# A graph layer on one core: edge blocks of 512 for a node range, and ten paired pairs in two regions

## What is computed

```python
h = relu(layernorm(x))                       # x: 3125 nodes x 64
msg = concat(h[dst], edge_attr)              # 53125 edges, sorted by dst
m = relu(msg @ W1a.T + b1a) @ W1b.T + b1b    # 128 hidden
agg = segment_sum(m, src) / max(count(src), 1)
z = relu(concat(h, agg) @ W2a.T + b2a) @ W2b.T + b2b
out = x + concat(z, h) @ Wr.T + br
```

## Time and profile before

| | us |
|---|---|
| time, median of 3 runs | 522.17 (521.17 to 524.77) |
| span of the profiled execution | 518.3 |
| TensorE busy | 431.0 (83%) |
| GpSimd busy | 356.1 (69%) |
| VectorE busy | 298.0 (57%) |
| ScalarE busy | 285.0 (55%) |
| moved by DMA | 123.45 MB, mean 238 GB/s |

### The profile page before, as it was taken

One profiled execution on the slowest core, in us unless ns is written; L12 is line 12 of the kernel. 1 busy time (PEld: TensorE's weight loads), 2 busy tenths in 40 slices (PEclk: granted clock), 3 DMA queues, 4 the chain that ended last, 5 costly groups with the idle time before them and its releaser, 6 DMA issues.

```text
span 518.3 us, 9203 instructions
## 1 busy us (share of the span) xinstructions
PE 431.0 (83%) x3133; PEld 390.0 (75%) x3133; DVE 298.0 (57%) x825; ACT 285.0 (55%) x576; POOL 356.1 (69%) x406
## 2 busy tenths in 40 slices
PE   6655988899999999998689779845999787987795
PEld 4555777888796988878578778845998777987674
DVE  7868642534656657555425547414765537667884
ACT  3442957774787777786658378171633772100073
POOL 4777777777677777777777777777777777776000
PEclk9876696987999899988899889986999897999999
DMA  7998998553959477978553989996999997778631
GB/s 182 306 338 229 257 266 271 155 156 108 303 143 294 141 257 265 257 255 263 164 151 92 336 249 333 312 331 196 360 326 336 328 322 221 248 214 256 177 86 43
DMA packets 62319, 123.45 MB, mean 238 GB/s; under 512 B 9369, under 2 KB 33374, under 8 KB 62270
## 3 DMA queue, kind: packets, MB, share of 16 engines
q1 hardware_dynamic: 49598, 91.25, 59.0%
q0 software_dynamic: 12672, 31.58, 18.8%
HBM read 71.53 MB, written 51.25 MB: 237 GB/s over the span
## 4 chain that ended last, share of the span: by engine, by line
POOL 32%; PE 26%; DMA 13%; issue 13%; DVE 7%; ACT 5%; SPq 2%; POOLq 0%; ACTq 0%; DVEq 0%
POOL slots_dram L568 24%; PE bank L1261 10%; POOL pairs_dram L551 8%; DMA slots_dram<-pay,pos_i 7%; PE bank L1241 4%; PE bank L1270 4%; DMA dstb<-in_dst 4%; DVE oh L774 2%; DMA rows<-slots_dram 2%; ACT eo L1059 2%; SPq L475 1%; PE bank L1294 1%; PE bank L1291 1%; PE bank L1211 1%; PE bank L1362 1%
## 5 line engine op out<-in xcount | busy, mean ns | idle before, releaser
L568 POOL DMA_INDIRECT slots_dram<-pay,pos_i x300 | 289.0, 963 | 98.7 <-issue 89.6
L1261 PE MATMUL bank<-rows,oh 128*125 128x130 f32 x1100 | 139.5, 287 | 40.3 <-DVE oh L774 40.1
L1261 PEld LDWEIGHTS bank<-rows,oh 128*125 128x125 f32 x1100 | 133.3, 198 | 44.6 <-issue 43.4
L1059 ACT ACTIVATE eo<-dstb,minus_lane 64x256 f32<-64x256 int32 x190 | 85.1, 494 | 94.5 <-DMA dstb<-in_dst 79.8
L1241 PE MATMUL bank<-pw,eo 128*128 128x128 f32 x856 | 119.9, 299 | 3.5 <-ACT pay L1042 2.3
L1241 PEld LDWEIGHTS bank<-pw,eo 128*128 128x128 f32 x856 | 113.3, 213 | 11.4 <-issue 8.0
L774 DVE TENSOR_TENSOR oh<-bank,rows 128x1500 f32<-128x1500 f32 (+5 forms) x67 | 81.8, 1223 | 17.6 <-DMA rows<-slots_dram 10.4
L1270 PE MATMUL bank<-hid,xch 116*128 116x131 f32 (+1 forms) x512 | 68.3, 294 | 14.6 <-DVE xch L724 8.6
L1270 PEld LDWEIGHTS bank<-hid,xch 116*128 116x128 f32 (+1 forms) x512 | 65.3, 205 | 16.9 <-issue 9.9
L551 POOL DMA_INDIRECT pairs_dram<-pay,pos_c x64 | 61.5, 960 | 22.3 <-issue 18.0
L1064 ACT ACTIVATE eo<-eo,one 64x512 f32<-64x512 f32 x95 | 68.3, 719 | 3.1
(11 more groups left out here) (198 smaller groups left out, 376.7 us busy)
## 6 DMA issues: line engine op xcount, KB each, us to landing
rows<-slots_dram SPq DMA_DIRECT2D x24, 864.0 KB
dstb<-in_dst SPq DMA_DIRECT2D x54, 256.0 KB, 7.7
eo<-in_edges_T SPq DMA_DIRECT2D x54, 256.0 KB, 4.9
rows<-pairs_dram SPq DMA_DIRECT2D x12, 864.0 KB
slots_dram<-zeros SPq DMA_DIRECT2D x9, 756.0 KB, 9.2
slots_dram<-pay,pos_i POOLq DMA_INDIRECT x300
rows<-slots_dram SPq DMA_DIRECT2D x8, 432.0 KB
rows<-slots_dram SPq DMA_DIRECT2D x16, 216.0 KB
```

Of the source, the lines that this page charges most:

```text
L568: pool.indirect_dma_start(out=slots_dram[:, :], out_offset=bass.IndirectOffsetOnAxis(ap=pos_i[:, u, k:k + 1], axis=0), in_=pay[:, u, k, :] ...
L1059: last = A.activation(eo[p, g % EB, a * HB:(a + 1) * HB], dstb[p, g % DB // 2, a * HB:(a + 1) * HB], ACT.Square, bias=minus_lane[p, g // 2 ...
L1261: last = T.matmul(o[0:BN, v * SW:(v + 1) * SW], oh2[:, r % 2, n, :], rows[:, sum_no[r] % RR, n, 0:SW], start=(t == 0), stop=(t == TB[ph] - ...
```

## The change

A window serves a block of 512 edges (462 in a paired pair), so a group has 2 blocks in place of 4: half as many projection matmuls, half as many and twice as long one-hots, window copies of half the size. The windows still hold 64 nodes a group, and begin 18 and 22 nodes ahead in place of 26 and 30. Of the 27 pairs 10 are paired in place of 8, at every other place from pair 4 to pair 22 (g44, g45); three old pairs follow. The paired pairs have two regions of 5 pairs each, with 4 tiles a bucket each, where one region of 6 tiles a bucket was; the phases of old pairs are 5, 5, 3, 2, 1, 1, of 4, 4, 3, 2, 1, 1 tiles a bucket (4, 4, 4, 2, 1, 1 before). The last group has 7 tiles in place of 4. Each region is cleared and checked by itself; the check of a paired region stands behind its last `crank`. The shares of the plan are 25 and -4 in place of 23 and -8.

What the plan gives, counted from the code:

| | before | after |
|---|---|---|
| indirect DMAs, old tiles + paired units | 300 + 64 | 271 + 80 |
| projection matmuls | 108 | 54 |
| hidden matmuls | 428 | 431 |
| sum tiles (of these left over behind g53, without the tail's 25) | 550 (75) | 575 (91) |
| sum rounds left over (and 9 in the tail) | 18 | 20 |
| `h` rounds | g7, 2 in g8, g11, 3 in g12 | g7, 2 in g8, 2 in g9, 2 in g11 |
| `z` rounds | 2 in g12, g15, g19, g23, 2 in g27 | 2 in g11, 5 in g12 |
| sum tiles in groups with a `crank` | g31: 16 | g19: 24, g23: 12, g31: 24, g35: 12, g39: 12, g43: 24 |
| sum tiles in g14 to g37 | 16: 24, 20: 24, 24: 24, 28: 12, 31: 16, 36: 24 | 16: 24, 19: 24, 20: 24, 23: 12, 24: 16, 30: 24, 31: 24, 32: 24, 35: 12, 36: 28 |
| and in g38 to g45 | 39: 12, 40: 24, 41: 24, 42: 16, 43: 24, 44: 24, 45: 24 | 39: 12, 40: 24, 43: 24, 44: 24 |
| and in g46 to g53 | 24, 24, 24, 6, 24, 24, 24, 28 | 0, 13, 27, 27, 24, 24, 24, 24 |

The core of the diff:

```diff
-ORDER = "OOOO" + "CO" * 8 + "O" * 7
+ORDER = "OOOO" + "CO" * 10 + "OOO"
-    WS, HB = 64, 256
+    WS, HB = 64, 512
-    BLOCK = [HB if kind == "O" else UNIT for kind in ORDER]
-    LEAD = [26 if kind == "O" else 30 for kind in ORDER]
+    BLOCK = [HB if kind == "O" else 2 * UNIT for kind in ORDER]
+    LEAD = [18 if kind == "O" else 22 for kind in ORDER]
...
-    PAIRS = [5, 5, 5, 2, 1, 1]
+    PAIRS = [5, 5, 3, 2, 1, 1]
+    PAIRED = [5, 5]
...
-    C = [math.ceil((expected(ph) + 4 * math.sqrt(expected(ph))) / 128) for ph in range(NPH)]
+    C = [math.ceil((expected(ph) + 3.8 * math.sqrt(expected(ph))) / 128) for ph in range(NPH)]
...
-    TB = C + [2 * CT]
+    TB = C + [2 * tiles for tiles in CT]
...
-    AFTER_PHASE = [4, 4, 4, 2, 1, 0, 4]
+    AFTER_PHASE = [4, 4, 3, 2, 1, 0, 4, 3]
...
-    ROUNDS_FROM, FULL_FROM, EARLY_SHARE, SHARE, C_SHARE, MOST = 7, 10, 10, 23, -8, 32
+    ROUNDS_FROM, FULL_FROM, EARLY_SHARE, MOST = 7, 10, 10, 32
+    SHARES = dict(after_old=25, after_paired=-4)
...
+                for p in range(1, NCP):
+                    piece = len(CLEAR_PIECES) - (FIRST_PAIRED[p] - g) // 2
+                    if g % 2 == 0 and 0 <= piece < len(CLEAR_PIECES):
+                        clear_chunks(p, piece)
...
-                        pool.wait_ge(s_cfill, 16 * len(CLEAR_PIECES))
+                        pool.wait_ge(s_cfill[C_STARTS.index(c // 2)], 16 * len(CLEAR_PIECES))
...
-                split_row(c_parts, c_carry, 2 * SCALE * SCALE, S["cw"])
+                if n + 1 not in C_STARTS:
+                    split_row(c_parts, c_carry[:], 2 * SCALE * SCALE, S["cw"])
+                    return
+                p = C_STARTS.index(n + 1) - 1
+                check_chunks(p)
+                if p + 1 < NCP:
+                    split_row(c_parts, c_first[:, p + 1, :], 2 * SCALE * SCALE, S["cw"])
...
-                for c in range(KW):
+                for c in range(blocks_of(i)):
```

More of the change, by code:

```diff
@@ L86, in gnn_layer @@
     CU = UNITS * len(C_GROUPS)
[L87 to L93, removed]
+    c_mean = [2 * UNITS * pairs * (UNIT / NB / 2 + 0.25) for pairs in PAIRED]
+    c_dev = [math.sqrt(2 * UNITS * pairs * (UNIT / NB / 4 + 0.0625)) for pairs in PAIRED]
+    CT = [math.ceil((c_mean[p] + 3.8 * c_dev[p]) / 128) for p in range(NCP)]
+    C_CAP = [tiles * 128 for tiles in CT]
+    C_BEGIN = [CR * UNITS * 128 + NB * sum(C_CAP[:p]) for p in range(NCP)]
+    C_ROOM = [min(C_CAP[p], 32 * math.ceil((C_CAP[p] - c_mean[p] + 4.5 * c_dev[p]) / 32)) for p in range(NCP)]
+    C_LEAST = [C_CAP[p] - C_ROOM[p] for p in range(NCP)]
+    assert all(0 < room <= 256 for room in C_ROOM)
+    C_SLOTS = C_BEGIN[-1] + NB * C_CAP[-1] + CU * 128
+    assert C_SLOTS < 2 ** 15
     HR, PR = 2, 4
@@ L137, in gnn_layer @@
     room = 0
-    for g in range(NG):
+    for g in range(LG):
         units = [("perm", C_GROUPS.index(g - 1), u, 0) for u in range(UNITS)] if g - 1 in C_GROUPS else []
@@ L165, in gnn_layer @@
     round_of = {n: r for r, n in sum_no.items()}
-    first_round = [min(r for r, v in enumerate(rounds) if v[0] == "sum" and v[1] == ph) for ph in range(NPH + 1)]
+    first_round = [min(r for r, v in enumerate(rounds) if v[0] == "sum" and v[1] == ph) for ph in range(NPH + NCP)]
     last_perm = [rounds.index(("perm", c, UNITS - 1, 0)) for c in range(len(C_GROUPS))]
@@ L344, in scatters_of @@
         def scatters_of(u, n):
-            return 16 * sum(KT[O_GROUPS[a]] for a in range(u, n, PB))
+            return 16 * sum(KT[O_GROUPS[a]] for a in range(u, min(n, len(O_GROUPS)), PB))
         def chunk_scatters_of(u, c):
@@ L460, in _ @@
             loaded = 0
-            for g in range(3, NG):
+            for g in range(3, LG):
                 if g >= 6:
@@ L539, in _ @@
             count(unit_row[:], [[1, K + 1], [0, 2]], 0, 0)
-            count(c_first[:], [[C_CAP, NB]], C_BEGIN, 0).then_inc(S["late"], 1)
+            for p in range(NCP):
+                last = count(c_first[:, p, :], [[C_CAP[p], NB]], C_BEGIN[p], 0)
+            last.then_inc(S["late"], 1)
             pool.wait_ge(S["pad"], 1)
-            for g in range(NG):
+            for g in range(LG):
                 if g in C_GROUPS:
@@ L1098, in _ @@
             copy_window(4)
-            for g in range(3, NG):
+            for g in range(3, LG):
                 relu(g)
-                if g + 2 < NG:
+                if g + 2 < LG:
                     copy_window(g + 2)
@@ L1297, in sum_round @@
                     pe.wait_ge(S["bc"], 1)
[L1298 to L1299 removed]
+                    for a in range(2):
+                        last = T.transpose(o[0:1, a * NBK:(a + 1) * NBK], col_stat[:, a:a + 1], I[0:NBK, 0:NBK])
                 last.then_inc(S["ag"], 1)
```

126 lines of the change are left out of this document (68 added, 58 removed).

## The result

The changed kernel takes 563.36 us (median of 4, 560.58 to 565.31), the kernel before beside it 521.67 (520.62 to 524.77): a ratio of 1.0787, 95% interval 1.0741 to 1.0833. A later run of both gave 1.0836 (1.0766 to 1.0906). Slower, as forecast, but by 42 us and not by 15: 563 lies outside the range of 510 to 547. Times are medians of all runs of a kernel, while ratios leave out single runs that lay over 1.5% above the kernel's fastest, so a ratio can differ from the quotient of the medians, in e16 by 0.9%.

What follows compares the result with a forecast made beforehand. Before, GpSimd's indirect DMAs were taken as the bound; after, TensorE paces: 137.9 + 269.6 + 0.5 = 408.0, GpSimd's last DMA at 492.7, tail 40.3, span 533.0, with 3.9 about 537 us measured. Range 510 to 547.

Steps and rivals of the forecast that it cites:

- what becomes the bound: g14 to g45: TensorE paces eight cycles at 33.7 us each against GpSimd's 30.3, 269.6 in all; chance 0.62.
- Rival (a): GpSimd stays the bound, faster, with VectorE's work behind the crank covered: measured 510 us; chance 0.22.
- Rival (b): About the same: waits are there, but no clock loss and the early rounds covered: measured 521 us; chance 0.12.
- Rival (c): DMA queues pace the kernel, with 5.3 MB more to move: 22 us on the old span, measured 544; chance 0.03.
- Rival (d): The range check fails on the tighter windows and the slow path runs, thousands of us; chance 0.01.
- GpSimd's price of a unit: On GpSimd, a paired unit costs what an old tile costs, 960 against 963 ns, so 13 fewer DMAs save 16.4 us.
- the windows: On TensorE, 54 projection matmuls in place of 108 take 16.4 us in place of 32.8.
- the size of the waits: g14 to g45: TensorE idles 34.0 us for one-hots, 27.6 of it six waits of 4.6 behind cranks; bounds 17 and 34.
- the clock term: g14 to g45: slow matmuls behind six crank waits lose 1.6 us each, 9.6 in all; bounds 0 and 9.6 + 6.
- the copies in g28 and g29: TensorE outruns ScalarE's unit copies in these groups without sums; 1.7 us idle, with cheaper one-hots, where 2.41 was.
- the early step: Up to g13: moved h and z rounds end g13's permutations 4.2 us later, at 137.9; bounds 0 and 8.
- the tail: From GpSimd's last DMA to the span's end: stays 40.3 us, 3.6 more for left-over tiles and 3.8 given back.

Runs made afterwards that it cites:

- e16: The changed kernel with e4's h and z rounds, e1's order and nine pairs (regions of 5 and 4); 743.46 us, ratio 1.0031 to the kernel before.
- e1: The changed kernel with VectorE making the one-hots of a sum round right behind a crank before taking the crank's results; 544.97 us, ratio 1.0431.
- e3: The changed kernel with a plan that puts no sum round into a group with a crank, leaving 187 tiles over; 547.68 us, ratio 1.0521.
- e8: The kernel before with e1's edit, which has one such place, g31; 520.73 us, ratio 0.9996.
- e2: The changed kernel with only the 512-edge block kept, and pairs, region, phases, shares and plan as before; 520.63 us, ratio 0.9985.
- e5: The changed kernel with TensorE's waits before seven sum rounds filled by 40 or 20 identity transposes, order unchanged; 552.31 us, ratio 1.0567.
- e4: The changed kernel with the h, z and window-check rounds in the groups where the kernel before has them; 557.17 us, ratio 1.0662.
- e7: The changed kernel with e4's plan and e1's order, and no sums in g31 and g43, leaving 127 tiles over; 543.45 us, ratio 1.044.
- e10: The changed kernel with 128 more already-met waits at the start of TensorE's program; 747.56 us, one run, against 738.93 for the kernel before.
- e9: The changed kernel with 64 more already-met waits at the start of TensorE's program; 746.81 us, one run, against 738.93 for the kernel before.

## Why the prediction was right in sign and wrong in size

**Right: what becomes the bound.** TensorE paces g14 to g45, GpSimd waits for `pos_c`, and the cause is a sum round behind a crank. e1 and e3 take the cause away in two ways and win 18.4 and 15.7 us; e8 shows that it costs nothing before the change. Rival (a), GpSimd stays the bound, fell, since GpSimd waits for `pos_c` in eight of the ten pairs; e3 shows it could have held for GpSimd alone. Rival (b), the waits without a clock loss and with the early rounds covered, fell by both: 18.6 us behind the waits, and g13's units 9.5 us later than before. Rival (c), the queues: 128.64 MB at a mean of 229 GB/s, lower than before's 238, and e3 moves the same bytes and GpSimd has no wait behind g13. Rival (d): a slow path would be thousands of us.

**Right: GpSimd's price of a unit.** 963 ns for a paired unit, 967 for an old tile, by the page above, with twice the bytes. The Trainium skill ("DMA: Bandwidth & Descriptors", anatomy of the GpSimd path) would, as an estimate, make the larger DMA as a whole dearer by 0.17 us; GpSimd's own time for it doesn't show that.

**Right: the windows.** 54 projections take 19.1 us in place of 32.8, where I had 16.4, so 13.7 us went and not 16.4; e2 shows that by themselves they bring nothing.

**Right: the size of the waits.** 34.0 was predicted for the one-hots in the stretch, 35.4 measured (the eight above and 1.49 in g32). Single places fit too: g23 5.59 and g43 5.17 for 5.5 with the region checks ahead, g30 2.11 for 2.2, g16 2.41 for 2.4.

**Wrong: the clock term, in the cycles.** I took "six times 1.6: 9.6", from one place with 16 tiles. It is 18.6 in eight places, 2.3 each. Two things were wrong in that term. I priced the six waits behind a crank and not the two of 2.4 and 2.1 us (g16, g30), though I had both in the sum of waits; they lost 1.8 and 1.7. And I took the loss of one place where the slow clock held for a part of a round; at others it held for nearly all of it (12 tiles in 5.33 is close to half speed throughout). With 9.0 of the 14.7 us missed in the cycles, 7.7 from start to start, this is the largest part of the miss, and e5 gives the clock a run of its own: some 11 us of the end time. The Trainium skill ("TensorE: Matmul & The Clock Gate", the part on the HAM clock gate) puts the warm-up under 1% of a typical span, at most 5.2 us as an estimate. The slow rounds behind these eight waits cost 18.6 us, 3.3% of this span (17.3 and 3.1% from start to start). As a bound for all of them together, as the prediction took it, the 1% does not hold here, and it would have led further off than my own term.

**Wrong: the copies in g28 and g29.** Predicted 1.7; measured 4.1 of waits and 1.8 of slow matmuls behind (3.72 for 1.96). This is TensorE's timeline there:

```profile
251.65 1.16 PE L1270 MATMUL bank<-pw,eo 128*128 128x128 f32 x8 [0.82 <-ACT hid L1071]
252.64 1.96 PE L1299 MATMUL bank<-hid,xch 116*128 116x131 f32 x16
257.88 3.72 PE L1299 MATMUL bank<-hid,xch 116*128 116x131 f32 x16 [3.28 <-ACT pay L1100]
```

I argued from ScalarE's cheaper one-hots that the wait would shrink from 2.41 to 1.7. It grew. That the order of ScalarE's work is behind it, with TensorE further ahead, fits e5, where the waits for the copies in g28 and g29 grew again, from 3.3 to 5.8, when TensorE came earlier; no run changes ScalarE's order, so it is not shown. With the clock's 9.0, this 4.2 and 1.4 of waits make 14.6 of the 14.7, or 13.3 with the clock taken from starts.

**Wrong: the early step.** "I take their net cost there as nothing (bounds 0 and 3.8)", of the two `h` rounds in g9. The upper bound was right. TensorE, 85 to 104 us:

```profile
89.61 2.07 PE L1299 MATMUL bank<-hid,xch 116*128 116x131 f32 x16 [1.20 <-ACT pay L1100]
91.52 3.89 PE L1320 MATMUL bank<-wl,hT 65*125 65x64 f32 x16
95.20 3.73 PE L1270 MATMUL bank<-pw,eo 128*128 128x128 f32 x16
98.72 1.06 PE L1218 MATMUL bank<-we_in,hT 65*128 65x128 f32 x4
99.57 4.44 PE L1299 MATMUL bank<-hid,xch 116*128 116x131 f32 x32
```

The 3.89 us of `h` rounds stand ahead of the hidden matmuls and permutations of g10, and those run cold (3.73 where 1.95 is usual, 4.44 for 3.8), while the wait of 1.52 that they were to fill is simply gone. The permutations end at 104.01, where they ended at 100.28 in the kernel before. So 3.7 of the 5.3 us missed are these two rounds. Of the other 1.6 the largest piece in the timeline is a wait of 1.04 us for VectorE ahead of the first `z` rounds, at 112.27; the rest is not split. e4 gives 6.2 back in the end, and 8 us at g13, which is my 4.2 and the missed 5.3 less 1.5.

**Wrong: the tail.** "The tail stays 40.3": it is 49.1. That 16 more left-over tiles (3.6 us) would be given back by GpSimd's later end was an argument without a row, and it failed: 3.1 of them came (38.2 against 35.1), and e3 and e7 show about the same price, 0.25 and 0.21 us a tile (27.9 / 112 and 7.5 / 36). The other 5.6 us lie behind the last instruction of VectorE, where TensorE's sequencer comes late to the closing line. No row of before hinted at it, and I had no bound for it. In all eight traces of ten-pair kernels taken beside a kernel before of 521 the wait is 6.8 to 7.1, with eight pairs 1.6 (before), 1.7 (e2) and 1.3 (e8). The table of DMA queues has, for the last 14 us, four instruction transfers on the queue q14 in the ten-pair kernels and one or two with eight pairs (on q8 two or three in both). That could be the program's loading, but it is not shown: the cause stays open.

**Why the range missed.** Its upper end, 547, was the sum of my own bounds for the early step and "other slow spots", and it had no room for the tail nor for errors that add: 5.3, 14.7 and 8.7 are all of one sign. The first two are not independent: a slow clock is part of both (the hidden matmuls and permutations of g10, the rounds behind the waits).

## What to carry to other kernels

Taking work from the engine that sets the time pays only as far as the next one has room, and waits in its program order that cost nothing before then cost time: the same edit is free at the one place in e8 and worth 18 us at the places in e1. Price each such wait twice on TensorE, by its length and by the slow matmuls behind it (here 33.9 and 18.6 us). For a wait of some 2 us the second price has two values: 1.7 and 1.8 in the changed kernel, nothing behind three such waits in e1. And follow displaced work to its new place: e3 gave GpSimd all its gain and lost more than that to 112 tiles moved into a tail in which nothing hides them.

## What the runs showed of the hardware that I had not expected

- Waits of 2.1 and 2.4 us were followed by matmuls at reduced speed (7.00 and 7.18 for 5.34, the granted clock 0.50 in the first 2 us), 1.7 and 1.8 us lost where waits of 4.6 us lost 2.1 to 2.7. It isn't so each time: behind waits of 2.04, 2.08 and 2.28 us in e1 twelve tiles took 2.90, full speed. What decides it was not tested. Filling the waits with matmuls of no use, here transposes, took the loss away at all seven places.
- A closing wait of 6.9 us for TensorE's sequencer, 5.3 more than before, which shifts of 64 and 128 instructions, nine pairs or one region did not bring to 2, all of them tried only where the kernel before took some 735. What causes it stays open.
- Where TensorE stopped for up to 6.3 us within its sum rounds with no releaser (e10; 5.6 in e9), everything tried stood at 1.003 to 1.036 of the kernel before, the changed kernel at 1.011 in two single runs: the margins of this document were measured with a TensorE that isn't held up.
